# Second attention of a macaron block: pair maxima on 64-row tiles, unrolled groups, neighbouring score matmuls

## What is computed

```python
q, k, v = _rope(proj(Wq)), _rope(proj(Wk)), proj(Wv)      # 16 heads of 16 channels
scores = einsum('bhsd,bhtd->bhst', q, k) / sqrt(256)
scores = where(causal_mask, scores, -inf)
o = einsum('bhst,bhtd->bhsd', softmax(scores), v)
out = o @ Wo.T
```

## Time and profile before

| | before |
|---|---|
| median of 3 runs | 2342.56 us (2339.42 to 2347.28) |
| profiled execution, its own time | 2343.61 us |
| its span, first to last instruction | 2341.8 us |
| mean granted TensorE clock | 0.934 |
| busy share of the span: PE, DVE, ACT, POOL | 87%, 72%, 43%, 42% |

### The profile page before, as it was taken

How to read it: one execution, slowest core, us unless ns; L and a number is a source line. 1 busy time by engine, 2 the same in 40 slices (tenths; PEclk the granted TensorE clock), 3 DMA queues, 4 the chain that set the end, 5 groups by cost and what they waited for, 6 DMA issues and landing times. The chain is left out here.

```text
span 2341.8 us, 36616 instructions
## 1 busy us (share of the span) xinstructions
PE 2037.0 (87%) x10632; PEld 1205.8 (51%) x10632; DVE 1676.4 (72%) x3188; ACT 1000.3 (43%) x2042; POOL 975.4 (42%) x865
## 2 busy tenths in 40 slices
PE   4757999999999999999999999567699998999996
PEld 3634555555555555555555554455454554554545
DVE  6667877878778778687787784775586785767825
ACT  1223343443434434434434434111167666666771
POOL 0023685795775856956957766013300000000000
PEclk8867999999999999999999999678799999999998
DMA  2200000000000000000000000110000000000001
GB/s 84 65 8 5 8 1 5 9 1 5 8 1 12 1 5 8 1 5 8 1 5 0 1 1 0 39 39 23 1 1 1 1 1 1 2 2 1 1 1 37
DMA packets 19790, 23.26 MB, mean 10 GB/s; under 512 B 4128, under 2 KB 17952, under 8 KB 19488
## 3 DMA queue, kind: packets, MB, share of 16 engines
q1 hardware_dynamic: 18416, 20.00, 2.8%
q10 hardware_dynamic: 1200, 1.31, 0.2%
HBM read 19.21 MB, written 2.10 MB: 9 GB/s over the span
## 5 line engine op out<-in xcount | busy, mean ns | idle before, releaser
L1100 ACT ACTIVATE lath_probs<-lath_shifted 128x512 f32<-128x512 f32 (+3 forms) x640 | 357.8, 565 | 683.3 <-DVE lath_shifted L1211 650.5
L1177 POOL TENSOR_TENSOR lath_summed<-lath_summed,lath_probs 128x512 f32<-128x512 f32 (+3 forms) x528 | 584.6, 1128 | 122.4 <-ACT lath_probs L1100 112.4
L1211 DVE TENSOR_TENSOR lath_shifted<-lath_score,lath_shift 128x512 f32<-128x512 f32 (+3 forms) x640 | 385.3, 607 | 147.8 <-PE lath_score L986 131.5
L1218 DVE TENSOR_REDUCE lath_maxima<-lath_max 128x1 f32<-128x512 f32 (+3 forms) x640 | 380.3, 605 | 132.4 <-PE lath_max L1007 84.8
L1623 DVE TENSOR_REDUCE atth_maxima<-atth_max 128x1 f32<-128x512 f32 (+3 forms) x640 | 355.1, 605 | 98.2 <-PE atth_max L1746 54.2
L1702 ACT ACTIVATE atth_probs<-atth_score 128x512 f32<-128x512 f32 (+3 forms) x640 | 313.6, 536 | 178.4 <-PE atth_score L1760 92.0
L994 PE MATMUL lath_out<-lath_probs,lat_latent 128*64 128x512 f32 (+3 forms) x1280 | 307.2, 559 | 0.0
L1007 PE MATMUL lath_max<-lat_key_hi,lath_query_hi 128*128 128x512 f32 (+3 forms) x640 | 266.0, 424 | 18.0 <-DVE lath_maxima L1218 16.5
L1746 PE MATMUL atth_max<-atth_key,atth_query 128*128 128x512 f32 (+3 forms) x640 | 267.3, 429 | 15.1 <-DVE atth_query L1595 6.2
L982 PE MATMUL lath_score<-lath_query_hi,lat_key_hi 128*128 128x512 f32 (+3 forms) x640 | 265.9, 415 | 4.0 <-DVE lath_shifted L1211 4.0
L1760 PE MATMUL atth_score<-atth_query,atth_key 128*128 128x512 f32 (+3 forms) x640 | 246.6, 407 | 14.0 <-ACT atth_probs L1702 11.6
(11 more groups left out here) (341 smaller groups left out, 2839.3 us busy)
## 6 DMA issues: line engine op xcount, KB each, us to landing
ffn_a_w<-in_L_ffn_W SPq DMA_DIRECT2D x2, 1024.0 KB, 11.7
lat_raw_out<-in_L_attn_w_out SPq DMA_DIRECT2D x8, 256.0 KB, 2.7
lat_rope<-in_c_rope_feature SPq DMA_DIRECT2D x1, 2048.0 KB, 10.8
ffn_b_w<-in_L_ffn_W SPq DMA_DIRECT2D x2, 1024.0 KB, 7.6
mix_a_factors<-in_L_ffn_factors SPq DMA_DIRECT2D x8, 256.0 KB, 4.1
out<-x SPq DMA_DIRECT2D x4, 512.0 KB, 2.9
lat_raw_q<-in_L_attn_w_q_b SPq DMA_DIRECT2D x8, 192.0 KB, 2.4
x<-in_L_attn_x ACTq DMA_DIRECT2D x2, 512.0 KB, 7.0
```

The source lines that it names most:

```text
L1100: nc.scalar.activation(probs[:, prob_slot(j, kt), h, q0:CH], shifted[:, 2 * (kt % 2) + h, q0:CH], ACT.Exp, scale=SCALE0).then_inc(s["exp_d ...
L1177: last = nc.gpsimd.tensor_tensor(summed[:, j % 2, h, q0:CH], so_far, probs[:, prob_slot(j, kt), h, q0:CH], ALU.add)
L1211: nc.vector.tensor_tensor(shifted[:, 2 * (kt % 2) + h, q0:CH], score_bank[score_place(j, kt, h) % 3][:, q0:CH], shift[:, j % 2, h, q0:CH], ...
L1218: nc.vector.reduce_max(maxima[:, h, i, kc:kc + 1], max_bank[(i * (nj + 1) + kc) % 2][:, 0:width], AX.X).then_inc(s["maxima_taken"], 1)
```

## The change

The functions that made the old order are replaced by `attention_plan`, one list of events for all 16 chunks (`CHUNKS`: three groups in order j = 0 to 3, the last group in order 3 to 0). There is no hardware loop; every wait is on a constant.

Maxima and scores now use 64-row tiles: `query` holds a pair of heads like `key`, with no zero halves, and each matmul takes 64 rows of the array (`rows_of(h)`). The two heads of a pair are issued next to each other, into two banks. For maxima a pair of banks is a `slot` (two slots in all), and one VectorE reduction takes both heads. The slots also serve all transposes, eight at a time, which had a bank of their own. On the diagonal, the four 128x128 triangles of a pair lie in one slot with one mask matmul a head; the rest of the diagonal chunk has no mask. The two scores of a pair stand behind one wait on the exponentials. Scores on the diagonal are not masked before the exponential; GpSimd zeroes the upper triangle of the result (`affine_select`, 64 of them). The copies of the high parts and of v move from ScalarE to GpSimd. Keys, v and several small tiles get two buffers.

```diff
+QUERY_TILES = 4
+STEP_TIME = 2.45
+LAST_GROUP = NCH * (NG - 1)
+CHUNKS = [(g, j) for g in range(NG - 1) for j in range(NCH)] + [(NG - 1, j) for j in reversed(range(NCH))]
...
+def maxima_jobs(j):
+    for pair in range(2):
+        yield pair, "triangle", 0, ((0, CH),)
+        yield pair, "odd", 0, ((1, P), (3, 3 * P))
+        yield pair, "even", 0, ((2, 2 * P),)
+        for i in range(TPC):
+            for kc in range(j):
+                yield pair, "whole", kc, ((i, CH),)
...
+    for n, (g, j) in enumerate(CHUNKS):
+        begin = max(maxima_end, ended[n - QUERY_TILES] + 3.0 if n >= QUERY_TILES else 0.0)
+        others.append((begin - 6.0, ("split_queries", n)))
+        jobs.append((begin - 1.3, 1.2, ("queries", n)))
+        if n <= LAST_GROUP:
+            for m in range(n, n + 1 if n < LAST_GROUP else NCH * NG):
+                ahead = 0.0 if n < LAST_GROUP else 8.0 * (NCH * NG - 1 - m)
+                others += [(begin - 6.0 - ahead, ("split_keys", m)), (begin - 5.0 - ahead, ("copy_values", m))]
+                jobs.append((begin - 2.6 - ahead, 1.3, ("keys", m)))
+        at = begin
+        for k, job in enumerate(maxima_jobs(j)):
+            jobs.append((at, 0.0, ("maxima", n, k, *job)))
+            at += 0.18 * len(job[3]) + sum(width for _, width in job[3]) / 480
+        maxima_end = at
+        jobs.append((at + 1.6, 1.2, ("shifted", n)))
+        step_end = max(step_end, at + 4.5)
         for kt in range(key_tiles(j)):
...
+            length = STEP_TIME * (0.2 + 0.8 * (CH - max(kt - TPC * j, 0) * P) / CH)
+            others += [(step_end + 0.25 * (h - h % 2) * length, ("scores", n, kt, h, len(step_ends))) for h in range(GROUP)]
+            if kt >= TPC * j:
+                others.append((step_end + 0.99 * length, ("mask", n, kt, len(step_ends))))
+            step_end += length
+            step_ends.append((step_end, n, kt))
+        ended.append(step_end)
+    for step, (end, n, kt) in enumerate(step_ends):
+        at = min([end + LAG * STEP_TIME, *(e - 0.01 for e, _, _ in step_ends[step + LAG:step + LAG + 1])])
+        others.append((at, ("values", n, kt, step)))
+        if kt == key_tiles(CHUNKS[n][1]) - 1:
+            others.append((at + 1.2, ("drain", n)))
+            jobs.append((at + 2.6, 0.6, ("finish", n)))
+    jobs.sort(key=lambda job: job[0])
+    out, taken, last = [], [-100.0, -100.0], -100.0
+    for r, (at, delay, event) in enumerate(jobs):
+        last = at = max(at, taken[r % 2] + 0.01, last + 0.01)
+        taken[r % 2] = at + delay
+        out.append((at, (event[0], event[1], r, *event[2:])))
+        if event[0] != "maxima":
+            out.append((taken[r % 2], (event[0] + "_out", event[1], r)))
+        elif event[2] == MAXIMA_JOBS[CHUNKS[event[1]][1]] - 1:
+            out.append((at + 0.001, ("shift", event[1])))
+    return [event for _, event in sorted(out + others, key=lambda e: e[0])]
...
-        v_one = sb("v_one", [P, NT, GROUP, 32])
-        key = sb("key", [P, 2, TOKENS], F32R)
-        query = sb("query", [P, NCH, GROUP, CH], F32R)
-        maxima = sb("maxima", [P, GROUP, TPC, NCH])
-        row_max = sb("row_max", [P, GROUP, TPC])
+        v_one = sb("v_one", [P, 2, NT, GROUP, 32])
+        key = [sb(f"key{n}", [P, 2, TOKENS], F32R) for n in range(2)]
+        query = sb("query", [P, QUERY_TILES, 2, CH], F32R)
+        maxima = sb("maxima", [P, 2, GROUP, TPC, NCH + 1])
+        row_max = sb("row_max", [P, 2, GROUP, TPC])
         probs = sb("probs", [P, 4, GROUP, CH])
-        out_t = sb("out_t", [P, CH])
-        inverse = sb("inverse", [P, TPC, GROUP])
+        out_t = sb("out_t", [P, 2, CH])
+        inverse = sb("inverse", [P, 2, TPC, GROUP])
-        max_bank = [ctx.enter_context(nc.psum_tensor(f"atth_max{i}", [P, CH], F32)) for i in range(3)]
+        slot = [ctx.enter_context(nc.psum_tensor(f"atth_slot{i}", [P, 2, CH], F32)) for i in range(2)]
...
+                    elif kind == "maxima":
+                        r, k, pair, what, kc, parts = a
+                        if k == 0:
+                            wait_taken(pe, place["keys", keys_before(n) - 1])
+                            wait_taken(pe, place["queries", n])
+                        if what == "triangle":
+                            for h in range(2):
+                                nc.tensor.matmul(slot[r % 2][:, h, :], core.ident_b, core.mask_qk.unsqueeze(1).broadcast_to([P, TPC, P]),
+                                                 start=True, stop=False)
+                            for i in range(TPC):
+                                for h in range(2):
+                                    own = slice(j * CH + i * P, j * CH + (i + 1) * P)
+                                    last = nc.tensor.matmul(slot[r % 2][:, h, i * P:(i + 1) * P],
+                                                            query[rows_of(h), n % QUERY_TILES, pair, i * P:(i + 1) * P],
+                                                            key[g % 2][rows_of(h), pair, own], start=False, stop=(i == TPC - 1))
+                        else:
+                            begin = 0
+                            for i, width in parts:
+                                first = (kc if what == "whole" else j) * CH
+                                for h in range(2):
+                                    last = nc.tensor.matmul(slot[r % 2][:, h, begin:begin + width],
+                                                            query[rows_of(h), n % QUERY_TILES, pair, i * P:(i + 1) * P],
+                                                            key[g % 2][rows_of(h), pair, first:first + width], start=True, stop=True)
+                                begin += width
+                        last.then_inc(s["filled"], 1)
+                    elif kind == "scores":
+                        kt, h, step = a
+                        u = GROUP * step + h
+                        if kt == 0 and h == 0:
+                            wait_taken(pe, place["shifted", n])
+                        if h % 2 == 0:
+                            wait(pe, s["exp_done"], u - 1)
+                        q0 = queries_from(kt, j)
+                        nc.tensor.matmul(score_bank[u % 3][:, q0:CH], key[g % 2][rows_of(h), h // 2, kt * P:(kt + 1) * P],
+                                         query[rows_of(h), n % QUERY_TILES, h // 2, q0:CH], start=True, stop=True).then_inc(s["scores_done"], 1)
...
+                    elif kind == "maxima":
+                        r, k, pair, what, kc, parts = a
+                        dve.wait_ge(s["filled"], r + 1)
+                        heads = slice(2 * pair, 2 * pair + 2)
+                        if what == "triangle":
+                            nc.vector.reduce_max(maxima[:, n % 2, heads, :, 0], slot[r % 2][:].rearrange("p h (t k) -> p h t k", t=TPC), AX.X)\
+                              .then_inc(s["taken_by_vector"], 1)
+                        else:
+                            begin = 0
+                            for i, width in parts:
+                                at = 2 + kc if what == "whole" else 1
+                                nc.vector.reduce_max(maxima[:, n % 2, heads, i, at], slot[r % 2][:, :, begin:begin + width], AX.X)\
+                                  .then_inc(s["taken_by_vector"], 1)
+                                begin += width
...
+                    elif kind in ("queries_out", "shifted_out"):
+                        r, = a
+                        act.wait_ge(s["filled"], r + 1)
+                        nc.scalar.activation(query[:, n % QUERY_TILES], slot[r % 2][:], ACT.Copy).then_inc(s["taken_by_scalar"], 1)
...
+                        nc.gpsimd.tensor_copy(part(q_slot, n, 1), part(q_slot, n, 0))
+                        nc.gpsimd.tensor_tensor(part(q_slot, n, 2), by_head(qk, g, j), part(q_slot, n, 0), ALU.subtract).then_inc(s["q_split"], 1)
...
+                    elif kind == "mask":
+                        kt, step = a
+                        q0 = queries_from(kt, j)
+                        pool.wait_ge(s["exp_done"], GROUP * (step + 1))
+                        own = probs[:, step % 4, :, q0:q0 + P]
+                        nc.gpsimd.affine_select(own, own, [[0, GROUP], [1, P]], ALU.is_ge, 0.0, base=0, channel_multiplier=-1)\
+                          .then_inc(s["masked"], 1)
```

471 lines of the change are left out of this document (161 added, 310 removed).

## The result

The changed kernel takes 2389.49 us (median of 4 runs, 2386.09 to 2393.79), against 2344.04 us (2339.42 to 2347.28) for the kernel before on the same chip: a ratio of 1.0196 (95% interval 1.0171 to 1.0221), 45 us slower where 110 us faster were predicted. The stage took 632.5 us before. In the profiled execution it now runs from 1652.8 to 2330.8 us, 678 us, and nothing outside it moved in this execution. The forecast for it was 522 us, so 156 us have to be found.

What follows compares the result with a forecast made beforehand. TensorE was taken to bound the steps. First group 106 us, its chunk 3 43, three groups 311, additions 58, tail 4: stage 522 us instead of 632.5, kernel 2232 us; own range 2165 to 2260, 8 in 10 2165 to 2300.

Steps and rivals of the forecast that it cites:

- rivals 1 and 2: Score pairs: heads not side by side, 2293 us, chance 0.22; 64-row tiles not streaming, 2493 us at 0.40, chance 0.06.
- The step: Full step on TensorE: values, two score pairs and two maxima jobs, one of them hidden, take 2.85 us.
- rival 4: GpSimd's mask on the diagonal is slow: at 3 us each it adds 50 us, 2282 us; chance 0.05.
- what is added to the steps: Turns, triangle masks and ScalarE copies at each chunk: 4.5 us a chunk, between 0 and 8; 58 us for 13 chunks.
- slots and not exponentials set the pace: Sign that the forecast is wrong: TensorE waiting mostly for VectorE's reductions; no size given.
- the first group: Group 0: 10 us to first maximum, VectorE's 87, late jobs 6, shift 3; chunk 3's scores start at 106 us.
- first score at about 20 us: Sign that the forecast is right: the stage's first score starts at about 20 us.
- rival 3: TensorE's clock falls to its low level: 67 us if three steps in ten do, 2299 us; chance 0.08.

Runs made afterwards that it cites:

- copies at once: Changed kernel, with copies out of turned slots planned 0.05 us behind the turn's start instead of at the slot time's end: 2280.28 us, 0.9732.
- without steps in between: Copies at once, with group 0's maxima ahead of its steps and 128-row zero matmuls on TensorE until the first values: 2311.41 us.
- the best version: Copies at once, with a wait for each score instead of one per pair, and 128-row zero matmuls until the first values: 2265.37 us, 0.9673.
- The same without filling: Copies at once, with a wait for each score instead of one per pair and no zero matmuls: 2273.02 us, 0.9706.
- the filling: Changed kernel with 128-row zero matmuls where TensorE is about to wait: 2370.45 us, 1.0104; with 64 rows 2388.89 us, 1.021.
- the copies early: Changed kernel, copies out of turned slots planned 0.4 us behind the turn's start: 2326.55 us, 0.9922; with 128-row zero matmuls added 2335.19 us, 0.9961.
- both truer step times: STEP_TIME 2.45 to 2.85 on the changed kernel: 2390.47 us; 2.45 to 2.65 on copies at once with a wait for each score: 2290.07 us.

## Why the prediction was wrong

**Right.** Pairs run side by side: rivals 1 and 2 are out. By the Trainium skill (TensorE: Matmul & The Clock Gate, Part 3), matmuls on distinct row groups run concurrently. This trace agrees: a pair costs 0.23 us in a stream and 0.33 behind a values block, as a single 128-row matmul does. The step is 2.84 us against 2.85, the first product comes 10 us into the stage as taken. GpSimd's masks are hidden (rival 4 is out). VectorE's work was 370 us against 348 (four groups of 87), 6% more.

**The step that failed first: what is added to the steps.** The prediction charged 4.5 us a chunk for turns, triangle and ScalarE's copies, "between 0 (all hidden) and 8". It summed durations and shared them out as hidden or not. From the start of chunk 3 of group 0 the 13 chunks last 160 us longer than their plain steps (2.85, and 8.85 for a diagonal), 12.3 us a chunk, above its own upper bound. With copies at once, the same instructions and TensorE's order unchanged, they last 71 us longer, 5.5 a chunk. So the 4.5 us for durations were nearly right once the order was mended, and the order was not looked at: the prediction never asked, for each copy, what stands ahead of it in its engine's order, and whether that waits for TensorE work that itself queues behind the slot. It listed the sign ("slots and not exponentials set the pace") and priced no rival by it. The old kernel had a bank of its own for the turns and three for maxima; the new one has two slots for both, so one late copy stops both. No run gave the turns a slot of their own, so what the merging by itself costs isn't shown.

**The second: the first group.** Forecast for chunk 3's scores 106 us into the stage; 156.8 measured, 140.0 with copies at once. So the late copies make 17 us of the 51. The rest, in steps from kernel to kernel (each of the profiled execution, so good to a few us): without steps in between and with the clock at 0.97, VectorE reaches the shift at 103.5 us, against 97. With steps in between and little time at the low level, in the best version, it does so at 120.1, so the steps delay it by 17 us, not 6. The same without filling has it at 125.1 (the low clock, 5 us), and with the single wait for a pair at 130.4 (another 5). From the shift to the score it is 9.5 us, not 3: the shift, its turn and its copy each wait in a queue. The sign "first score at about 20 us" failed with it: 31.4 us in the change.

**The clock (rival 3).** It came true in size, 259 us at the low level, and was priced at 67 us for three steps in ten. But most of it is a consequence: with the copies at once (0.92 over 572 us) some 95 of the 259 us are left. By itself, and net of the filling's own cost, the clock is worth 19 us where the filling took 137 us of the low level away in the change, nothing with the copies early, and 15 us in the first group without steps. The split between ring and clock is not exact: a turn at the low clock takes 1.97 us instead of 1.09 and so makes its slot late, and a late slot idles TensorE. The runs bound it; they don't separate it.

The sum: 522 us forecast, 51 for the first group, 105 for the rest of the stage (of which 102 are in the added work of the 13 chunks and the others in its end), 678. With the copies at once it is 572 us, and 2280 for the kernel: 48 above the forecast, inside the range for 8 in 10 (2165 to 2300) and outside the forecast's own (to 2260). So 106 of the 156 us are the places of the copies, with the clock that follows from them; some 34 of the other 50 lie in the first group.

Open: which order of TensorE's own jobs would be best (both truer step times failed to help), and how much of the 17 us that the steps cost the first group a third slot would save; that was not tried.

## What to carry to other kernels

When an order is written out for several engines, a copy that gives back a shared buffer has to stand in its engine's order right where its input is ready, ahead of anything that needs a later product; moving it by 1 us in the plan was worth 109 us here, more than twice what the rewrite had lost. Such places can be counted in the orders before anything runs. Charge side work not by its duration times a share that is hidden, but by walking one chunk boundary through the queues: what is in front of each release, and what that waits for. Before merging rings (two slots for turns and maxima instead of four banks), check that a late release of one kind can't stop the other.

## What the runs showed of the hardware

- Two 64-row fp32r matmuls of 512 columns on the two halves of the array hold TensorE 0.23 us together in a stream and 0.33 behind a values block, the same as one with 128 rows (0.24 and 0.33).
- With 64-row matmuls one at a time the granted clock was 0.56 and 0.67 over the stage, and 0.51 and 0.55 over stretches of 150 us in which TensorE was busy 95 to 100%; the kernel before, with 128 rows, had 0.96 over the stage. Zeros multiplied on 128 rows raised the clock in the changed kernel from 0.81 to 0.91, on 64 rows to 0.86.
- A 64-row product followed by a 128-row mask and back cost 0.47 us where the 128-row product and mask took 0.25.
- GpSimd's affine select of 128x512 took 0.64 us, less than half of the 1.465 us of its tensor operation of that size.
